# Shared expert's tokens turned by DMA from the two-byte table, and the router moved into the shared expert's groups

## What is computed

```
x = x + attn(layernorm(x))          # 4 heads without softmax
x = x + xattn(layernorm(x), ctx)    # softmax attention over a context
y = layernorm(x)
logits = y @ router_w + router_b; probs = softmax(logits); the 2 best of 16 experts per token
pos = number of earlier picks of the same expert (a running count over all tokens)
slot = expert * 640 + pos, dropped where pos >= 640
x = x + y + mlp_shared(y) + sum over the two experts of gate * mlp_expert(y)
mlp(h) = (silu(h @ wg) * (h @ wu)) @ wd        # 512 -> 704 -> 512
```

## Time and profile before

| | |
|---|---|
| median of 3 runs | 1907.94 us |
| profiled execution | 1906.54 us, its span 1904.8 us |
| PE busy | 98% |
| DVE, ACT, POOL busy | 45%, 38%, 45% |
| granted clock, mean | 0.995 |

### The profile page before, as it was taken

One profiled execution on the slowest core, in us unless ns is written; L12 is line 12 of the kernel. 1 busy time (PEld: TensorE's weight loads), 2 busy tenths in 40 slices (PEclk: granted clock), 3 DMA queues, 4 the chain that ended last, 5 costly groups with the idle time before them and its releaser, 6 DMA issues.

```text
span 1904.8 us, 27457 instructions
## 1 busy us (share of the span) xinstructions
PE 1866.0 (98%) x10352; PEld 1642.1 (86%) x10352; DVE 861.2 (45%) x1976; ACT 726.2 (38%) x1446; POOL 847.8 (45%) x727
## 2 busy tenths in 40 slices
PE   8999999999989999999999999999999999999997
PEld 5788888888877778888899999999999999999996
DVE  2575577568554322222324444344444344443442
ACT  3344444454452211111334444434444344444331
POOL 2133253344365220000456656666556566566631
PEclk9999999999999999999999999999999999999998
DMA  8003312321454432233665666666666767666622
GB/s 275 10 9 125 133 40 94 133 80 55 144 181 134 106 68 67 67 81 85 135 148 137 145 129 161 152 143 148 133 143 157 150 140 144 131 157 155 144 45 28
DMA packets 191603, 224.36 MB, mean 118 GB/s; under 512 B 99664, under 2 KB 99664, under 8 KB 191216
## 3 DMA queue, kind: packets, MB, share of 16 engines
q1 hardware_dynamic: 166176, 169.51, 30.8%
q0 software_dynamic: 25296, 53.11, 16.0%
HBM read 135.92 MB, written 65.68 MB: 106 GB/s over the span
## 4 chain that ended last, share of the span: by engine, by line
PE 67%; DVE 1%; ACT 1%; issue 0%; POOL 0%; ACTq 0%; DVEq 0%; POOLq 0%
PE ps L71 45%; PE ps L1353 22%; ACT buffer L1161 0%; DVE buffer L1247 0%; ACT buffer L381 0%; DVE buffer L1264 0%; DVE stats L512 0%; ACT lg L442 0%; PE ps L722 0%; ACT buffer L1203 0%; PE ps L728 0%; POOL out_tokens L1150 0%; ACT L1203 0%; DVE oh L682 0%; DVE buffer L658 0%
## 5 line engine op out<-in xcount | busy, mean ns | idle before, releaser
L71 PE MATMUL ps<-buffer,buffer 128*128 128x320 f32 (+1 forms) x6816 | 1224.2, 341 | 7.4 <-DVE buffer L623 2.1
L71 PEld LDWEIGHTS ps<-buffer,buffer 128*128 128x128 f32 x6816 | 1106.5, 188 | 110.8 <-DVE buffer L623 2.3
L1102 POOL TENSOR_TENSOR buffer<-buffer,buffer 128x512 fp32r<-128x512 f32 x289 | 390.4, 1514 | 210.6 <-ACT buffer L1161 210.2
L1353 PE MATMUL ps<-buffer,buffer 128*128 128x512 f32 x1904 | 439.1, 390 | 4.1 <-DVE buffer L1247 4.0
L1161 ACT ACTIVATE buffer<-buffer 128x512 fp32r<-128x512 f32 (+4 forms) x689 | 374.1, 595 | 172.5 <-PE ps L1353 90.9
L1353 PEld LDWEIGHTS ps<-buffer,buffer 128*128 128x128 f32 x1904 | 355.1, 188 | 82.3 <-issue 5.8
L1264 DVE TENSOR_TENSOR buffer<-ps,buffer 128x320 f32<-128x320 f32 (+1 forms) x240 | 127.5, 532 | 600.4 <-ACT buffer L1203 552.8
L1203 ACT ACTIVATE buffer<-ps 128x320 f32<-128x320 f32 (+1 forms) x240 | 112.5, 469 | 657.3 <-PE ps L71 628.5
L1150 POOL DMA_INDIRECT out_tokens<-buffer,slot_index x80 | 125.4, 1567 | 183.2 <-DVE buffer L1295 172.5
L1247 DVE TENSOR_TENSOR buffer<-buffer,buffer 128x320 fp32r<-128x320 f32 (+1 forms) x240 | 181.9, 758 | 12.0 <-ACT buffer L1161 10.7
L376 ACT ACTIVATE buffer<-ps 128x512 fp32r<-128x512 f32 (+1 forms) x212 | 112.6, 604 | 107.7 <-PE ps L71 44.2
(11 more groups left out here) (109 smaller groups left out, 890.9 us busy)
## 6 DMA issues: line engine op xcount, KB each, us to landing
buffer<-in_wts SPq DMA_DIRECT2D x289, 256.0 KB
tokens_normed_T<-buffer SPq DMA_DIRECT2D x16, 1024.0 KB
buffer<-tokens_normed_T SPq DMA_DIRECT2D x16, 1024.0 KB, 7.5
buffer<-in_x SPq DMA_DIRECT2D x8, 1024.0 KB, 6.8
buffer<-in_ctxT SPq DMA_DIRECT2D x8, 1024.0 KB, 12.8
out_tokens<-buffer SPq DMA_DIRECT2D x8, 1024.0 KB, 4.4
tokens_normed<-buffer SPq DMA_DIRECT2D x32, 256.0 KB, 3.3
out_tokens<-buffer POOLq DMA_DIRECT2D x32, 256.0 KB, 4.0
```

The costliest lines, as they stand in the source:

```text
L71: last = pe.matmul(out, left, right, start=(i == 0), stop=(i == len(todo) - 1))
L1102: pool.tensor_tensor(wl[n % RING][:], wraw[n % RAW][:], wh[n % RING][:].bitcast(F32), ALU.subtract).then_inc(s_wl, 1)
L1353: ins = pe.matmul(down_bank[n % 2][:], left, right, start=(c == 0 and i == 0), stop=(c == FC - 1 and i == len(passes) - 1))
```

## The change

Y2T and the DRAM tensor YT go. A step TURN issues 4 DMA transposes of 128 rows of the table Y each; a step TOK joins the halves (ACT the upper, DVE the lower, 4 tiles each) and then splits them (ACT `th`, DVE `tl`, 4 tiles each). LP and the gate and up products read `th`, `tl`. The whole router of every batch moves out of the first stage. SC uses banks 2 to 5 in order.

```
-    ahead = {"V": [("WEIGHTS", (0, 2))], "Q": [("WEIGHTS", (2, 6)), ("WEIGHTS", (6, 8))], "SC": [("LOAD", 0)],
-             "PT": [("WEIGHTS", (8, FIRST))]}
+    ahead = {"V": [("TURN", 0), ("WEIGHTS", (0, 2))], "Q": [("WEIGHTS", (2, 6)), ("WEIGHTS", (6, 8))], "PT": [("WEIGHTS", (8, FIRST)), ("TOK", 0)]}
...
-        steps = [("Y1T", i), ("V", i), ("ST0", i + 1), ("Y2T", i - 1), ("LN0", i + 1), ("INIT", i + 1),
-                 ("Q", i), ("G", i + 1), ("LP", i - 1), ("T", i + 1), ("LX", i - 1), ("L1", i - 1), ("L2", i - 1),
...
+        steps = [("Y1T", i), ("V", i), ("ST0", i + 1), ("LN0", i + 1), ("INIT", i + 1), ("Q", i), ("G", i + 1),
+                 ("T", i + 1), ("WV", i + 1), ("QB", i + 1), ("SC", i), ("M", i + 1), ("PT", i),
+                 ("C", i + 1), ("A", i + 1), ("LN1", i + 1), ("PV", i), ("LN2", i)]
...
-    router = {(0, 1): [("X", B - 2)], (0, 2): [("Y2T", B - 1)], (0, 3): [("LP", B - 1)], (0, 4): [("LX", B - 1), ("L1", B - 1)],
-              (1, 0): [("L2", B - 1)], (1, 1): [("X", B - 1)]}
+    router = {(0, 0): [("LP", 0)], (0, 1): [("LX", 0), ("L1", 0)], (0, 2): [("L2", 0)], (0, 3): [("X", 0), ("TOK", 1)],
+              (0, 5): [("LP", 1)], (1, 0): [("LX", 1), ("L1", 1)], (1, 1): [("L2", 1), ("TOK", 2)],
+              (1, 2): [("X", 1), ("LP", 2)]}
+    scatter_after = {(0, 4): 0, (1, 3): 1}
+    for b in range(2, B):
+        if b >= 3:
+            router[b - 1, 1] = [("TOK", b)]
+            router[b - 1, 2] = [("LP", b)]
+        router[b - 1, 3] = [("LX", b), ("L1", b)]
+        router[b - 1, 4] = [("L2", b)]
+        router[b - 1, 5] = [("X", b)]
+        scatter_after[b, 0] = b
...
+            if name == "TURN":
+                if b == 0:
+                    sp.wait_ge(s_out, 16 * (B - 1))
+                    for stored in s_yout:
+                        sp.wait_ge(stored, 16 * NT * (B - 1) // 2)
+                for t in range(NT):
+                    sp.dma_start_transpose(turned(b, t)[:], Y[b * S + t * P:b * S + (t + 1) * P, :])\
+                        .then_inc(s_turn, 16)
...
+            if name == "TOK":
+                act.wait_ge(s_turn, 16 * NT * (b + 1))
+                for t in range(NT):
+                    copy(token_halves(b, t)[:, :, :, 1], turned(b, t)[:, 0:NC, :]).then_inc(s_ttop, 1)
...
             if name == "LP":
-                drained(pe, "Y2T", b, NC - 1)
...
+                pe.wait_ge(s_tl, NT * (b + 1))
...
         def load_tokens(g):
+            sp.wait_ge(attn["s_ttop"], NT * g)
+            sp.wait_ge(attn["s_tlow"], NT * g)
             if g >= 2:
                 sp.wait_ge(s_gu, unit_no[(g - 2, FC - 1, 0)] + 1)
...
+            step("TURN", g)
```

On SP the slot list is now read after all `load_tokens`; raw chunks 22 to 27 are loaded after `load_tokens(3)`. On POOL, DVE and SP the end of the shared expert becomes:

```
# GpSimd, in the loop over units: splits first, then
+                if (g, c) in scatter_after:
+                    step("SCATTER", scatter_after[g, c])
+                if (g, c) == (B - 1, 1):
...
+                    pool.wait_ge(s_index, 1)
+                    gather(B)
# VectorE, behind unit (7, 1)
+                    if (g, c) == (B - 1, 1):
+                        dve.wait_ge(s_list, 16)
+                        dve.tensor_copy(slot_index[:], slot_list[:, :, 0].bitcast(U32)).then_inc(s_index, 1)
# SyncE, behind load_tokens(7)
+        sp.wait_ge(attn["s_scat"], 16 * K * NT * B)
+        sp.dma_start(slot_list[:].rearrange("p (e t) k -> p e (t k)", e=E),
```

More of the change, by code:

```diff
@@ L177, in phase1, with token_rows, turned, token_halves @@
     halves_rows = [at(96, [2, D], U16), at(97, [2, D], U16)]
-    halves_last = [at(46 + t, [2, D], U16) for t in range(NT)]
+    halves_last = [at(row, [2, D], U16) for row in (38, 39, 48, 49)]
     def halves(b, t):
         return halves_last[t] if b == B - 1 else halves_rows[t % 2]
[L183 to L191, removed]
+    def token_rows(first, odd, even, shape, dt=F32):
+        parts = [at(row, shape, dt) for row in (first, odd, even)]
+        return lambda b: parts[0 if b == 0 else 1 if b % 2 else 2]
+    th, tl, tw = (token_rows(44, 52, 57, [NC, S], F32R), token_rows(40, 84, 62, [NC, S], F32R),
+                  token_rows(40, 84, 62, [NC, S]))
+    turned_first = [at(row, [2 * NC, P], U16) for row in (48, 49, 96, 97)]
+    turned_rows = [at(row, [2 * NC, P], U16) for row in (56, 61, 66, 94)]
+    def turned(b, t):
+        return turned_rows[t] if b else turned_first[t]
+    def token_halves(b, t):
+        return tw(b)[:, :, t * P:(t + 1) * P].bitcast(U16).rearrange("p c (n two) -> p c n two", two=2)
     ph, pl = y1h, y1l
@@ L572, in step @@
                 dve.tensor_tensor(rwp[:, :, E:2 * E], rw[:], rwp[:, :, 0:E].bitcast(F32), ALU.subtract).then_inc(s_rw, 1)
[L573 to L582, removed]
+            if name == "TOK":
+                dve.wait_ge(s_turn, 16 * NT * (b + 1))
+                for t in range(NT):
+                    dve.tensor_copy(token_halves(b, t)[:, :, :, 0], turned(b, t)[:, NC:2 * NC, :]).then_inc(s_tlow, 1)
+                for t in range(NT):
+                    cols = slice(t * P, (t + 1) * P)
+                    dve.wait_ge(s_th, NT * b + t + 1)
+                    dve.tensor_tensor(tl(b)[:, :, cols], tw(b)[:, :, cols], th(b)[:, :, cols].bitcast(F32),
+                                      ALU.subtract).then_inc(s_tl, 1)
             if name == "QB":
@@ L1121, in gpsimd @@
                     split(n)
-            elif name not in ("RAW", "LOAD"):
+            elif name not in ("RAW",):
                 step(name, b)
         for g, (job, part, tiles, last) in enumerate(groups):
-            if g + 1 < NG and groups[g + 1][0] > 0:
-                if g + 1 == B:
-                    for stored in attn["s_yout"]:
-                        pool.wait_ge(stored, 16 * NT * B // 2)
-                    pool.wait_ge(s_index, 1)
+            if g >= B and g + 1 < NG:
                 gather(g + 1)
```

139 lines of the change are left out of this document (43 added, 96 removed), and 3 rows, old and new, of the table BANK.

## The result

The changed kernel takes 1958.49 us (median of 4 runs, 1956.32 to 1959.66), the one before 1907.82 (4 runs, 1907.47 to 1910.38): a ratio of 1.026, 95% interval 1.0244 to 1.0279, so it is slower by 2.6%. The profiled execution spans 1957.0 us against 1904.8, 52.2 more; the forecast was 39.4 more.

| stretch | before, us | after, us | after - before | forecast |
|---|---|---|---|---|
| up to group 1 (start-up, middle and last iterations, group 0) | 639.26 | 614.67 | -24.6 | -26.3 |
| group 1 | 48.07 | 64.87 | +16.8 | +9.7 |
| groups 2 to 6 | 226.83 | 272.88 | +46.1 | +36.1 |
| group 7 | 47.75 | 63.95 | +16.2 | +19.9 |
| the experts | 942.9 | 940.6 | -2.3 | 0 |

The account below looks back on a forecast made before the run. PE, busy 98% of the span, was taken as the bound. Terms -26.0 - 0.3 + 9.7 + 36.1 + 19.9 = +39.4 us on the profiled 1906.54 gave 1945.9, as a median 1947.3; range 1914 to 1965.

Parts of the forecast that it names:

- rival D: Groups 1 to 6: the low clock comes there too, 2.9 us a drop; 1964 us, chance 0.07.
- rival E: TURN 0 and TURN 1: transposes from DRAM slower, delaying PT and LP by 5.5 us each; 1958 us, chance 0.06.
- Middle iterations: Iterations 1 to 6: each loses Y2T, LP, LX and X on PE, no new wait; 26.0 us off (20 to 26).
- Last iteration and group 0: Stage seam to group 1: earlier start against new waits before PT and LP and low clock; 0.3 us off.
- Groups 2 to 6: Router work and three new PE waits add 7.2 us a group, 36.1 us in all.
- PE's own work: Each group: LP, LX and X now run on PE there, 2.6 us a group.
- LP waits for TOK: Behind unit 2: TOK behind unit 1 takes 6.8 us, PE arrives at 5.4; 1.45 us a group.
- X waits for L2: Behind unit 5: `picked` from L2 behind unit 4 comes after PE ends unit 5; 1.85 us a group.
- down waits for `h_lo`: Down's first tile: DVE's other work makes unit 5's `h_lo` late, 1.3 us a group.
- I allow 1.4 and 1.0 us: Group 1: allowance for five splits beside L2 of batch 2, making the other two waits 3.3 and 2.3 us.
- Group 7: PE waits 11.4 us before unit 4 for the list, 5.4 in down, plus low clock; 19.9 us on (11 to 27).
- Rival C: Whole kernel: PE's saved work counts if `picked` and tokens are ready when PE comes; 1890 us, chance 0.10.

Follow-up runs that it names:

- e6_all: Changed kernel with all moves together: seam, TOK earlier, L2 and X later, early table load, batch 1, batch 7 and group 7 reordered; 1895.71 us, ratio 0.9921.
- e4_scatter_first: Changed kernel, but in group 7 POOL issues SCATTER 7 before unit 0's splits; 1944.98 us, ratio 1.0194 to the kernel before.
- e5_seam: Changed kernel, but SP issues weight loads 6 and 7 ahead of TURN 0 in the last iteration; 1953.94 us, ratio 1.0225 to the kernel before.
- e2_x_later: Changed kernel, X of batches 2 to 6 behind unit 0 of the next group, scatter behind unit 1; 1954.39 us, ratio 1.0242 to the kernel before.
- e3_tok_early: Changed kernel, TOK of batches 3 to 7 behind unit 0 instead of unit 1; 1949.7 us, ratio 1.0214 to the kernel before.
- e1_preload: Changed kernel plus one Silu on one column right behind the router's exponential, loading the table early; 1949.35 us, ratio 1.0209 to the kernel before.
- e10_memset_splits: Changed kernel, POOL's splits of 22 weight chunks, 17 to 38, replaced by memsets of zero; 1952.16 us, ratio 1.022 to the kernel before.
- e7_l2_x_later: Changed kernel, L2 of batches 2 to 6 behind unit 0 of the next group, X behind unit 1, scatter behind unit 2; 1932.13 us, ratio 1.0109.

## Why the prediction was right, and where its sizes were off

The forecast, slower through waits added in the groups, came true, and the time lies 11.5 us above it, inside the range. It lies nearer to rival D, 1964, and on the number of rival E, 1958; D's mechanism was there (part 3), E's was not: the four transposes of TURN 0 from DRAM took 6.01 us to issue (5.4 forecast), and PT waited less than forecast, not 5.5 us more. By its own parts:

1. **Middle iterations: right.** 28.0 us off for 26.0, no cover lost. The start-up ahead of them took 3.2 us more in this execution, part of it at a lower clock (0.87 for 1.00 in the product behind the wait of 2.06; Y1T of iteration 1 starts at 119.82 for 116.60); `e6_all` and `e4_scatter_first` have it at 116.6 and 116.4, so this is not the change's.
2. **Last iteration and group 0: right in all waits.** PT waited 6.64 (7.4 forecast), LP of batch 1 2.85 (3.1). The lower clock lasted 10.2 us from 539.2 and cost 3.3 (PT 3.67 for 1.97, PV 12.80 for 11.18, both beside `e5_seam`), where I had 1.9 and at most 2.9. Behind LP's wait it came again: LP and down took 1.7 us longer than in `e2_x_later`, where a wait of 2.82 brought no fall; forecast 1.4. Removing the first cause gave 4.6 us (`e5_seam`, medians). From Y1T of the last iteration to group 1 it is 116.89 us for 116.62, 0.3 on, where I had 0.3 off.
3. **Groups 2 to 6: the mechanism right, 7.2 us a group forecast, 9.2 measured.** The terms:

| term | forecast | group 5 | from |
|---|---|---|---|
| PE's own work | 2.6 | 3.0 | 48.31 - 45.33, `e6_all` |
| LP waits for TOK | 1.45 | 1.40 | row; gone in `e3_tok_early` |
| X waits for L2 | 1.85 | 3.07 | row; 1.78 in `e1_preload` |
| down waits for `h_lo` | 1.3 | 0 | 1.09 where the clock stays up |
| lower clock in down | 0 | 1.7 | 3.4 us at 0.51 |

The term that was mis-sized is X: I took the order and times of ACT from the earlier trace rows, a group in which no exponential stands between two Silus. The reload of 1.28 us starts only behind the wait for unit 4's gate, so it is wholly on the path; taking it out took 1.29 off the wait (`e1_preload`). The gap of 3.07 and not 1.8 then came with the lower clock in each group, rival D, which I had put at 0.07 and argued away with gaps of 2.2 and 1.5 us. Its price was smaller than I had it: 1.7 us and not 2.9, and about 0.6 of that net, since it hid the third wait, 1.09.

4. **Group 1: the step "I allow 1.4 and 1.0 us" failed.** X waited 7.1, not 3.3: the table reload, and 4.0 us of slow DVE instructions where I had allowed 1.4. LP waited 4.0, not 3.5, the 2.3 us for `h_lo` did not show, and the granted clock of the group was 0.89, for which I had nothing; it cost about 4 us (LP 3.62 for 2.04, the unit behind it 6.38 for 5.61, down 17.1 for 15.4). DVE's instructions of L2 stood behind splits of POOL. The Trainium skill has this rule (SBUF — State Buffer, SBUF: two separate sides): a DVE instruction with two inputs in SBUF and a GpSimd instruction that reads SBUF exclude each other on the port pair that the two engines share; the one that starts first keeps it for its whole length, and the other waits. The rows agree in the main: L676, L685 and `h_lo` (two SBUF inputs) are long, the product L1250 (one input from PSUM) is 0.69 throughout, and beside memsets, which read nothing, all three are normal. They differ in two points: the conversion L683 has one SBUF input and was long too (1.20), and `h_lo` in group 7 was held not by one split of 1.26 us but until the whole row was over (991.85 to 998.11, the row ending at 997.55). No run here explains either, and `e10_memset_splits` alone does not show that it is the port.
5. **Group 7: the first wait right, the second right in size by luck.** PE waited 8.89 for 11.4: SP issued the read of the list 26.9 us into the group, not 28, and it landed 3.0 us later, not 4. `e4_scatter_first` shows the splits ahead of the scatter as the cause: group 7 falls by 10.4 us. In down I had 5.4 us before the third tile; down's waits are 3.96 together, but there it is 0.52, because 3.44 us already went to `h_lo` behind POOL's splits (3.05 and 0.39), a wait that I did not have. Where `h_lo` is quick, the third tile waits 4.7 (`e10_memset_splits`). The lower clock cost 4.1 us (PE busy 49.72 for 45.61) for the 4 that I had.

**Rival C, faster, was a matter of order.** The chains that it needed short do not have to be short: they only have to end before PE comes. In groups 2 to 5 of `e6_all` two units of PE work stand between TOK and LP, and one whole unit between L2 and X, where half a unit (12 matmuls) stood; the kernel is 10.8 us of span under the one before. PE's saving, 28.0 + 1.7 in the iterations, less 3.0 a group for the router that it now does there, was real from the start; the waits and the clock cost 63.0 us of the changed kernel (1957.0 - 1894.0), 3.3 of them in the start-up.

What stays open: group 1 still takes 55.5 to 57.2 us in the best kernel, with up to 1.7 us before X of batch 1 and waits for `h_lo` in down of groups 0 and 1 (up to 2.4); no run was made for these. Nor was one made that tells the shared port from the length of POOL's instructions.

## What to carry to other kernels

When work is moved into gaps of another loop, write for each step who on PE reads it and which instruction that engine runs next, and leave more PE work between than the whole chain takes. One unit (5.4 us) was too little for TOK, a chain of 6.8 us, and half a unit for L2; two units and one unit were enough. A step on DVE delays two readers, its own and the one of whatever stands behind it; moving only the reader (`e2_x_later`) gained 2.2 us over groups 1 to 6, moving the step with it (`e7_l2_x_later`) 25.2. A change can hold a real saving (10.8 us of span) and lose nearly six times as much to its own order, so try the order before dropping the idea.

## What the runs showed of the hardware that I had not expected

- An activation table load of 1.28 us can stand behind the wait of the function that needs it, in each of the groups 1 to 6 behind 2.04 to 2.07 us of waiting, and so on the path. It does not always: in group 0 the load for the Silu of unit 2, which has one semaphore wait in the program and not two, ran ahead of its wait. No run shows whether that is the reason. The rows of group 0:

```profile
576.83 1.28 ACT L1191 ACT_TABLE_LOAD   x1
...
578.90 0.60 ACT L1191 ACTIVATE buffer<-ps 128x512 f32<-128x512 f32 x1 [0.79 <-PE ps L71]
```

  One Silu on one column right behind the exponential moves the load into the idle time (6.5 us less in groups 2 to 6, `e1_preload`).
- DVE's `h_lo`, with two SBUF inputs, stretched from 0.68 to 6.26 and 6.82 us (`e4_scatter_first`) beside POOL's splits in a row.
- The granted clock, 1.00 before, stood at 0.50 to 0.51 (the lower of its two levels) for 3.4 us behind an X wait of 3.07 in each of the groups 2 to 6. It fell in three of four groups with a wait of 2.52 (`e2_x_later`), in two of five with 1.78 (`e1_preload`), and in none with 0.94 (`e7_l2_x_later`, groups 2 to 5).
